# A fused norm, recurrence and gated cell on one core: gate f kept in SBUF, and a new order of the late units

## The reference, cut to what matters

```python
x = L0_attn_x                                   # 8 x 1024 x 256, fp32
h = _layernorm(x) * (1 + ca) + sa
# a recurrence over the 1024 steps, its output projected, added and normalised
h_t = tanh(h_{t-1} @ A.T + h[t] @ B.T);  y_t = h_t @ C.T
x = x + ga * (_layernorm(y + h) * gamma + beta)
h = _layernorm(x) * (1 + cb) + sb
# a gated cell; the batch is its time axis, c is carried over the 8 samples
ft = sigmoid(h @ wf.T + c @ uf.T + bf)
it = sigmoid(h @ wi.T + c @ ui.T + bi)
gt = tanh(h @ wc.T + c @ uc.T + bc)
c = ft * c + it * gt
x = x + gb * tanh(h @ wo.T + c_final @ uo.T + bo)
```

## Time and profile before

| | us |
|---|---|
| median of 3 runs | 561.13 (560.39 to 561.53) |
| the profiled execution | 560.83 |
| its span, first to last instruction | 559.0 |
| TensorE busy | 542.9 (97%) |
| VectorE busy | 389.9 (70%) |
| GpSimd busy | 342.5 (61%) |
| ScalarE busy | 342.1 (61%) |

### The profile page before, as it was taken

One profiled execution on the slowest core, in us unless ns is written; L12 is line 12 of the kernel. 1 busy time (PEld: TensorE's weight loads), 2 busy tenths in 40 slices (PEclk: granted clock), 3 DMA queues, 4 the chain that ended last, 5 costly groups with the idle time before them and its releaser, 6 DMA issues.

```text
span 559.0 us, 13427 instructions
## 1 busy us (share of the span) xinstructions
PE 542.9 (97%) x4620; PEld 532.6 (95%) x4620; DVE 389.9 (70%) x908; ACT 342.1 (61%) x862; POOL 342.5 (61%) x475
## 2 busy tenths in 40 slices
PE   6999999999999999999999999999999999999994
PEld 4899999999999999999999999999999999999983
DVE  6898878886767655565766776776677667665763
ACT  3777777775466555464755566666656556667551
POOL 4667777660376444354776666677666766678354
PEclk9999999999999999999999999999999999999999
DMA  7656445435243222222233333443333343232244
GB/s 267 187 189 200 141 151 152 133 97 154 90 139 104 72 71 79 74 67 77 59 107 103 105 102 96 116 124 102 96 95 96 96 127 108 87 101 90 63 117 153
DMA packets 58514, 64.10 MB, mean 115 GB/s; under 512 B 5408, under 2 KB 49736, under 8 KB 58448
## 3 DMA queue, kind: packets, MB, share of 16 engines
q1 hardware_dynamic: 58448, 63.26, 37.0%
HBM read 46.44 MB, written 16.81 MB: 113 GB/s over the span
## 4 chain that ended last, share of the span: by engine, by line
PE 83%; issue 5%; POOL 3%; DMA 3%; ACT 2%; DVE 2%; SPq 2%; POOLq 0%; DVEq 0%; ACTq 0%
PE psI L1573 13%; PE psOF L1573 13%; PE psG L1573 13%; PE psWR L1631 7%; PE psWR L1532 6%; PE psWR L1444 4%; PE psWR L1479 4%; PE psOF L1479 4%; PE psOF L1444 4%; PE psOF L1559 3%; PE psC L1559 3%; PE psT L1610 2%; DMA state<-in_L_wmod_dram 1%; PE psC L1496 1%; PE psT L1496 1%
## 5 line engine op out<-in xcount | busy, mean ns | idle before, releaser
L649 POOL TENSOR_TENSOR hin<-hin,uvec 128x256 f32<-128x256 f32 x64 | 50.8, 815 | 32.1 <-ACT hin L811 30.6
L656 POOL TENSOR_TENSOR hsl<-hs,hsh 128x512 fp32r<-128x512 f32 x24 | 31.0, 1291 | 49.1 <-DVE state L1284 32.6
L1268 DVE SCALAR_TENSOR_TENSOR lo<-psT,cb1T,hi 128x256 fp32r<-128x256 f32 x60 | 26.3, 479 | 48.9 <-ACT hi L876 48.9
L690 POOL TENSOR_TENSOR zn<-zn,tA 128x512 f32<-128x512 f32 x32 | 45.7, 1427 | 11.0 <-ACT zn L849 11.0
L849 ACT ACTIVATE zn<-state,nmA,rstdA 128x256 f32<-128x256 f32 x64 | 35.0, 594 | 26.3 <-POOL nmA L680 26.3
L1148 DVE TENSOR_TENSOR pre<-psWR,state 128x256 f32<-128x256 f32 x44 | 18.5, 420 | 45.9 <-PE psWR L1532 45.7
L1532 PE MATMUL psWR<-hs,AT 128*128 128x128 f32 x368 | 49.5, 274 | 0.0
L663 POOL TENSOR_TENSOR xin<-xin,tA 128x512 f32<-128x512 f32 x32 | 41.3, 1292 | 13.1 <-DMA tA<-rows_d 13.1
L838 ACT ACTIVATE hs<-pre 128x256 f32<-128x256 f32 x44 | 18.4, 417 | 50.6 <-DVE pre L1148 50.5
L1102 DVE SCALAR_TENSOR_TENSOR hin<-xin,mvA,uvec 128x256 f32<-128x256 f32 x56 | 41.1, 774 | 9.9 <-DMA h_park<-hin 9.5
L1532 PEld LDWEIGHTS psWR<-hs,AT 128*128 128x128 f32 x368 | 45.2, 191 | 0.1
(11 more groups left out here) (384 smaller groups left out, 2306.8 us busy)
## 6 DMA issues: line engine op xcount, KB each, us to landing
h_park<-hin SPq DMA_DIRECT2D x32, 256.0 KB, 2.2
hin<-h_park SPq DMA_DIRECT2D x64, 128.0 KB
xin<-in_L_attn_x_dram SPq DMA_DIRECT2D x64, 128.0 KB
tA<-rows_d SPq DMA_DIRECT2D x32, 256.0 KB, 4.5
out_dram<-state SPq DMA_DIRECT2D x64, 128.0 KB
xin<-in_L_attn_x_dram SPq DMA_DIRECT2D x28, 256.0 KB, 2.8
tW<-rows_d SPq DMA_DIRECT2D x32, 128.0 KB, 3.1
tG<-rows_d SPq DMA_DIRECT2D x24, 128.0 KB, 3.7
```

Of the source, the lines that this page charges most:

```text
L649: pool.tensor_tensor(h, h, sa, ALU.add).then_inc(a_h, 1)
L690: pool.tensor_tensor(two(zn[:, :]), two(zn[:, :]), both(tA[:, m % 2, 0:D]), ALU.mult).then_inc(s_zg, 1)
```

## The change

Gate f: ScalarE's sigmoid goes to `gf` in SBUF instead of back to psF; VectorE multiplies it there by c, and TensorE's next product for f waits for the sigmoid (s_f) alone. In unit 33 and later C's `project` stands behind gates f and g. At the turn in unit 34 `times_uo` stands where `times_wo` was, and `times_wo` at the unit's end. From unit 34 on (LATE2) `mean_var`, `ngA` and the factors of `zn` are made at the end of the unit before; GpSimd multiplies `zn` first and then the output, and adds `uvec` behind the factors of `xn`; ScalarE does `tanh_wx` behind `hi`, and `ngB` between gates i and g; without recurrence VectorE makes `row_stats` before the output's sum. The comparison of the ends stands two units earlier, its VectorE steps behind `clo`.

```diff
+    LATE2 = PAIRS + 2
 (GpSimd)
+            def factors_of_z(m):   # veA, rstdA, nmA as before
+            def scaled_out(o):     # the output times gb
+            def with_u(o):         # waits for s_wx, s_u; adds uvec
-                if norm:
-                    pool.wait_ge(s_mvA, 2 * m + 2)
...
+                if norm and u < LATE2:
+                    factors_of_z(m)
+                if has(o, 0, LAST) and (u < LATE2 or not norm):
+                    scaled_out(o)
                 if norm:
                     pool.wait_ge(s_zn, 2 * m + 2)
                     pool.tensor_tensor(two(zn[:, :]), two(zn[:, :]), both(tA[:, m % 2, 0:D]), ALU.mult).then_inc(s_zg, 1)
+                if u >= LATE2 and norm:
+                    scaled_out(o)
...
-                if has(o + 1, 0, LAST):
-                    if o >= 0:
+                if has(o + 1, 0, LAST) and (u < LATE2 - 1 or not norm):
+                    if u >= PAIRS and norm:
+                        pool.wait_ge(s_x1, m + 1)
+                    elif o >= 0:
                         pool.wait_ge(s_fin, o + 1)
+                    with_u(o + 1)
...
+                if u >= LATE2 - 1 and norm:
+                    with_u(o + 1)
+                    if m + 1 < NU:
+                        factors_of_z(m + 1)
 (ScalarE)
-                dst, src, fn, done = ((psF[:, :], psF, ACT.Sigmoid, s_f), ...
+                dst, src, fn, done = ((gf[:, :, :].rearrange("p m n -> p (m n)"), psF, ACT.Sigmoid, s_f), ...
-                if has(o, 0, LAST - 1):
+                if has(o, 0, LAST - 1) and u < LATE2:
                     tanh_wx(o)
...
-                    if m not in (1, 2):
+                    if m not in (1, 2) and u < LATE2:
                         ngA_of(m)
...
                     hi_of(n + 1)
+                if has(o, 0, LAST - 1) and u >= LATE2:
+                    tanh_wx(o)
...
                         gate(n, 1)
+                        if has(m, 1, NU - 1) and u >= LATE2:
+                            ng_of(m)
                         gate(n, 2)
...
+                if has(m + 1, LATE2 - ML, NU - LATE2 + ML):
+                    ngA_of(m + 1)
 (VectorE)
-                dve.tensor_tensor(gf[:, :, :], psF[:, :].rearrange("p (m n) -> p m n", m=H), prev, ALU.mult).then_inc(s_fc, 1)
+                dve.tensor_tensor(gf[:, :, :], gf[:, :, :], prev, ALU.mult).then_inc(s_fc, 1)
+                if u == PAIRS + 5:
+                    ... the four steps of the comparison, before `lo` (they were at PAIRS + 7)
+                if u == PAIRS + 7:
+                    ... the two steps to the flag (they were at PAIRS + 8)
+                if has(m, 1, NU - 1) and not rec:
+                    row_stats(m)
                 if has(o, 0, LAST):
                     dve.wait_ge(s_ob, o + 1)
                     dve.tensor_tensor(tiles_of(o), two(wx[:, o % NWX, :]), tiles_of(o), ALU.add).then_inc(s_fin, 1)
-                if has(m, 1, NU - 1):
+                if has(m, 1, NU - 1) and rec:
                     row_stats(m)
+                if has(m + 1, LATE2 - ML, NU - LATE2 + ML):
+                    mean_var(m + 1)
 (TensorE)
-                    pe.wait_ge((s_fc, s_c, s_g)[i], (n, n, 2 * n)[i])
+                    pe.wait_ge((s_f, s_c, s_g)[i], (2 * n, n, 2 * n)[i])
-                elif here:
+                elif here and u <= PAIRS:
                     project(here[0])
                 if x:
                     gate_x(n, 0)
                     gate_x(n, 2)
+                if here and u > PAIRS:
+                    project(here[0])
...
+                turn = has(n, NB, NU - NB) and n % NB == 0
+                if turn and not rec:
+                    times_uo(n // NB - 1)
+                if x and not rec and not turn and n < HELD:
                     times_wo(n)
...
-                if u == PAIRS + 8:
+                if u == PAIRS + 6:
                     pe.wait_ge(k_diff, 4)
...
-                if x and rec and n > 0:
+                if x and (rec or turn) and n > 0:
                     times_wo(n)
```

## The result

| | before | after |
|---|---|---|
| median of 7 runs | 561.17 us (560.39 to 561.70) | 562.99 us (562.39 to 564.23) |
| the profiled execution | 560.83 | 562.97 |
| its span | 559.0 | 561.1 |

The changed kernel is slower: the ratio is 1.0037, with a 95% interval of 1.0027 to 1.0047. The forecast was 560.2 us, and its range ended at 561.8.

What follows compares the result with a forecast made beforehand. TensorE, busy 542.9 of 559.0 us, was taken as the bound, so only its gaps and pace could be won. The turn's +0.4 and units 38 to 40's -1.3 took the median 561.13 to 560.2 us; range 557.9 to 561.8.

Steps and rivals of the forecast that it cites:

- The turn: Units 34 and 35: the wait for `uvec` goes, a new 1.6 us wait at gate g comes; net cost 0.4 us.
- The meeting of x1 with `scaled_out`: From unit 34 on, x1 on VectorE meets GpSimd's running output product and ends 0.9 us later.
- Gate f in SBUF: TensorE's waits for `gf` in units 38 to 40 go; the multiply meeting `with_u` in units 18 to 31 costs nothing.
- Units 38 to 40: 28.60 us before, 26.2 without waits: a gain of 2.4, less 1.2 of new waits, taken as 1.3 net.
- (b): TensorE from unit 38 to 39: gate f of unit 39 waits for `gf`; 1.2 us lost.
- (c): TensorE from unit 39 to 40: a wait by the same chain as (b), about 0.4 us from start to start.
- (d): Unit 40, gate i: c is late because the comparison of the ends stands before it; about 0.25 us.
- The comparison, costed at nothing in unit 37: Four VectorE steps, an estimated 1.6 us, push `lo` back 0.9 us in unit 37, but x1 ends where it did.
- No meeting on the port: Rival, chance 0.27: x1 and `scaled_out` don't meet; the turn gains 0.5, units 38 to 40 the full 2.4: 558.2 us.
- ngB holds gate g everywhere: Rival, chance 0.10: in units 35 to 39 ngB, ahead in ScalarE's queue, stalls gate g: 562.8 us.
- Nothing moves: Rival, chance 0.13: stalls shift between waits and a late `clo` eats the gain at units 38 to 40: 561.1 us.
- The pace: Matmul halves of unit 33 take 4.25 or 4.08 us; the new order moves this up to 0.8 us either way, nothing summed.

Runs made afterwards that it cites:

- e2: The changed kernel with GpSimd starting the output's product only when x1 is done, from unit 34 on: 560.41 us.
- e5: The kernel before with gate f's sigmoid in SBUF alone: 561.99 us.
- e9: The kernel before with only the new order of C and U, gate f in SBUF and the comparison two units earlier: 560.24 us.
- e7: The changed kernel with ngB behind gate g and GpSimd's output product after x1: 560.00 us.
- e16: e7 with the comparison of the ends one unit earlier still (VectorE in unit 36, TensorE in unit 37): 559.22 us.
- e12: e7 with `uvec` added to only two columns of each output tile from unit 37 on, the rest of that addition left out: 558.75 us.
- e1: The changed kernel with ngB behind gate g again in the late units: 563.26 us.
- e17: e7 with VectorE's sum with the bias (or the copy) ahead of the output's sum and gate f's multiply: 559.79 us.
- e18: e7 with both moves, the comparison as in e16 and the sum with the bias as in e17: 559.50 us.
- e15: e7 with the comparison of the ends back where the kernel before has it (units 39 and 40): 562.92 us.

## Why the prediction was wrong

**The turn: right.** +0.4 forecast, +0.35 measured. A wait of 1.6 us for gate g was named, with its chain; it lost 1.4. Its lower bound, a wait of 0.7 us and a gain of 0.5 without the meeting, is e2's 0.5 us and 0.57 (32.70 for 33.27).

**The meeting of x1 with `scaled_out`: right, and its price too.** From the `clo` of the earlier trace rows I took 0.9 us more; x1 took 1.61, 1.76, 1.63, 1.62 and 1.62 us in units 34, 35, 36, 38 and 39, where the earlier trace rows has 0.68. In unit 37 it was 0.68 (at 499.92), because the comparison had pushed it behind the other product.

**Units 36 and 37: right**, 20.33 us.

**Gate f in SBUF: the step "TensorE's waits go" was right, the step "I cost it at nothing" not.** In units 18 to 31 it indeed cost nothing in time that can be seen (unit 33 starts at 447.43 for 447.75). But it stretches rstdB in units 34 to 38 from 0.70 to 1.16, and e5 and e9, with the old order, where it stretches veB, pay 0.37 and 0.36 us a round for it (9.59 and 9.58 for 9.22).

**Units 38 to 40: wrong, by 3.2 us** (-1.3 forecast, +1.86 measured). The term that failed is "without waits they take 8.7 us each, so 26.2: a gain of 2.4". Part of it is size: the waits (b), (c) and (d) that I had read there make 1.85 us, not 2.4, and less its waits (1.2, 0.44 and 0.2 us) the stretch takes 26.8 us in before, as it does in after (30.46 less 3.7). The larger part, 2.5 us, is the waits: 3.7 us for `xn` and for gate g in place of 1.2 for c and `clo`. The term took for granted that the chain behind the waits for `gf` in the earlier trace rows was the only one as long, and subtracted small waits for c and `clo` from the gain. I had followed that chain inside one unit and never closed it. Closed, it stood in the trace of before: from nmA to nmA 9.22 us, the same as TensorE's unit 39 (511.38 to 520.61). The stretch can be cut at these two nmA into three terms, from unit 38's start to its nmA, the round, and from unit 39's nmA to unit 41:

| | to nmA | round | to unit 41 | sum |
|---|---|---|---|---|
| before | 4.05 | 9.22 | 15.33 | 28.60 |
| after | 4.94 | 10.38 | 15.14 | 30.46 |
| e7 | 4.66 | 9.62 | 14.37 | 28.65 |
| e16 | 3.97 | 9.62 | 14.37 | 27.96 |
| e12 | 3.30 | 8.93 | 14.73 | 26.96 |

The forecast's 27.3 was reached only by e12, which leaves work out. The first term is longer in e7 than in e16 by 0.69: the comparison in unit 37. The round is longer by 0.36 for gate f in SBUF (e9, e5); in e2 and e7, with the whole new order but x1 free, it is 0.40 longer, and the held x1 adds 0.75 (10.38 for 9.63 in e2). In the last term the change does gain, 1.0 us in e7; the held x1 takes 0.8 of it back. The forecast charged x1's 0.9 us to the turn and to c and `clo`, but not to `xn`, whose factors come behind it.

**The comparison, costed at nothing in unit 37: wrong.** Its steps meet GpSimd's products and take 3.5 us, not 1.6; `lo` came at 499.13, 3.4 us behind `clo`'s end. In units 38 to 41 this costs 0.7 us (28.65 in e7, 27.96 in e16).

**The rivals.** *No meeting on the port* gave 558.2; e2, which is that case, ran 560.4. It rested on the same 2.4 us for units 38 to 40, of which e2 gained nothing. *ngB holds gate g everywhere* was closest in its time (562.8) but not in its cause: e1 takes ngB away from gate g and gains nothing. *Nothing moves* is what e9 and e5 show of their parts, though not by a late `clo`: waits shift from `gf` to `xn`.

**The pace** of the matmuls gave no net part: stretches without waits are equal in both (20.33 and 20.34 us).

What stays open: how much of the 0.2 to 0.6 us by which units 38 to 41 get shorter in the profiles of e17 and e18 is won in time; the differences are within what these runs can tell. And no run separates the parts of the new order (the factors a unit ahead, the order on ScalarE, the order on VectorE) from one another.

## What to carry to other kernels

Where a stage repeats, close the chain that ends a wait: follow it from an instruction to the same instruction one unit later, over all engines and their queues, and compare the round with the bound engine's work per unit. While the round is longer than that work, a wait that is taken away comes back elsewhere, and the gain is what the round gets shorter by. The round need not be any one engine's own work: in the changed kernel GpSimd is busy for 8.1 of its 10.38 us, less than TensorE's products need, and still each of its steps on the chain counts in full. Add up the chain with the stretched durations, not the busy time of an engine.

## What the runs showed of the hardware

- Not only long products are held where VectorE and GpSimd meet. GpSimd's steps on 128x2 numbers went from 0.20 to 0.55 or 0.74 (veB, beside the output's sum) and from 0.70 to 1.16 (rstdB, beside the multiply for `gf`). With gate f back in PSUM rstdB is never over 0.702.
- A tensor_scalar with one input in SBUF, 0.29 us alone, took 1.27 beside GpSimd's `xin` addition. The Trainium skill, "SBUF — State Buffer", Who interferes with whom, says that `tensor_scalar` can enter a mode with both ports, when its operands meet some conditions, and then contends with GpSimd; this row agrees. The tensor_reduce behind it stayed at 0.42.
- TensorE's clock: after 3.5 us with 0.24 us of work the granted clock was 0.50 (the 1.2 GHz level) for 6.2 us, and matmuls of 256 columns went at 0.213 us (12 from 474.70 to 477.26) instead of 0.113 to 0.118. After the 1.4 us pause of the changed kernel it stayed at 1.00. Here a pause of 3.5 us so cost about 3.1 us more behind it (6.20 x 0.50), and in e15 3.33 us at 0.51, behind 2.40 us with 0.58 us of work, cost 3.33 x 0.49 = 1.6 us.
